# Another order of the steps on all five engines, and PSUM banks that go round the whole program

## The chip, the cores and the metric

The kernel runs on one core of one Trainium2 chip. Five engines work side by side, each through its own list of instructions in order: TensorE (PE in the profile; its weight loads are PEld), VectorE (DVE), ScalarE (ACT), GpSimd (POOL) and SyncE (SP), which here issues every DMA. An instruction starts when the one before it on its engine has gone and the semaphores that it names have reached their values. The metric is the time of one execution in microseconds (us).

## The reference

The input x is 16 batches of 512 tokens by 256 features, float32. For each batch:

```python
xn = layernorm(x)                                   # no gain, no bias
s  = attn(xn)                                       # 16 heads of 16 features
g  = silu(ffn(xn))
x  = x + s * g

# attn, for one batch
v = x @ v_w + v_b
wts = top8_softmax(mean_over_tokens(x) @ gate_w + ...)      # 16 heads x 16 waves
kern = sum(wts * sum(amps * sin(freqs . positions + phases)))
causal_kern = 3.0 * step(kern) * window                     # one row of 512 lags per head
scores = causal_kern[i - j] + qm[i] + km[j] + 0.15 * (qc . kc) / sqrt(8)
ctx = softmax(causal(scores)) @ v
h = layernorm(x + ctx @ out_w + out_b) * g1 + b1
return layernorm(h + gelu(h @ ffn_w1 + b) @ ffn_w2 + b) * g2 + b2

# ffn: three linear layers whose operands are first rounded to FP4 in blocks of 16
h = silu(q(x) @ q(w_gate).T) * (q(x) @ q(w_up).T)           # 704 wide
return q(h) @ q(w_down).T
```

The batches meet nowhere. What they share is prepared once: the statistics and the token means of all 16 batches (all of x has to be read for them), the kernel rows of every head and batch, and the three rounded weights.

## The kernel before

The program has no loop at run time. Python writes every engine's instructions out, from the table ORDER: a list of step names for each engine in three parts. The part `head` opens the program (steps `pre:` once for all, `pro:` for batch 0 ahead of time, `first:` for batch 0), `mid` is written out 14 times for batches 1 to 14, and `end` holds batch 15 (`last:`) and what is left after it (`tail:`). The order of a list is the order on that engine; nothing else schedules.

One batch goes through three stages that overlap with its neighbours. Names in the order lists are those of the code's branches:

- xT, proj, v make the transposed tokens, the split query and key parts and the values of the next batch. SP's `splitio` and `load` send the parts to DRAM and read them back in another layout.
- mx (40 uses of a bank in a batch) finds each row's maximum ahead of time: TensorE at L624, VectorE at L1037. mfin and mT turn the maxima into bias rows.
- sc.p.u is a piece of the scores of head pair p (L654 and L658). ScalarE takes the exponential (L822, L833); VectorE multiplies the near blocks by the kernel row (muld, L1067), GpSimd the far ones (mul, L1176). pv (L674) is the product with the values, ctxe and ctxt normalize it.
- xq, xr, gu, silu, hq, hr, tr, dn are the FP4 network: gu at L701, the rounding on VectorE at L923 to L941 and on GpSimd at L1215 and L1217, tr at L711, dn at L718.
- cT (L725), out (L733), ln1, lnc1, lnb1 (L980), hT (L750), f1 (L760), the Gelu on ScalarE (L913), f2 (L769), ln2 (L958), lnc2, lnb2 and fin end the batch before: they run one batch late.

In the opening, `px.n` loads batch n of x into one of four buffers, `st.n` and `cp.n` take its statistics on VectorE, and `sum` (L1541) adds its token means on TensorE, which frees the buffer for px.n+4. The last sum is L1546. After it comes a chain: pooled, gl, topk, wide, kern (L1585), tanh, soft (L1515 to L1520), the exponential at L1672 and the DMA of the kernel rows. `busy` (L1608) are matmuls of no use that keep TensorE going.

PSUM has eight banks. Scores use 0 and 1. The rest are two rings: 6 and 7 for xT, proj, v, mx and mT (49 uses in a batch), 2 to 5 for all else (56 uses). psum_plan gives each use the next bank of its ring and notes which use had it before; TensorE waits for that one's reader.

Of the kernel before, what the change touches and what calls it, by code (L numbers as in the profile page):

```python
# [56 lines left out]
class Event:  # L57
# [5 lines left out]
    def wait(self, eng, b, k=None):  # L63

        if isinstance(b, int) and b < 0:
# [18 lines left out]
            pro:projm.2 pre:wm.0.0 pre:rs.6 pre:rs.7 pre:rs.8 pre:rs.9 pre:rs.10 pre:wm.0.1 pre:rs.11 pre:rs.12
            pre:wm.1.0 pre:rs.13 pre:rs.14 pre:rs.15 pre:wm.1.1 first:xnb pro:xq pre:wm.2.0 pre:wm.2.1 pro:xr first:xq
            first:projm.0 first:projm.1 first:xr first:projm.2 first:mul.0 first:mul.1 first:hq.0 first:mul.2
            first:hr.0 first:mul.3 first:hq.1 first:mul.4 first:hr.1 first:hq.2 first:mul.5 first:hr.2 first:mul.6
            first:hq.3 first:mul.7 first:hr.3
# [1647 lines left out]
```

How the kernel before makes its waits and increments, by code:

```python
    def wait(self, eng, b, k=None):  # L63
        if isinstance(b, int) and b < 0:
            return
        k = self.per - 1 if k is None else k
        eng.wait_ge(self.sem, b * (self.per * self.by) + (k + 1) * self.by)
# [352 lines left out]
        def inc(ins, name):  # L421
            ins.then_inc(E[name].sem, 1)
# [56 lines left out]
        def sync_steps(sp, part, at_batch):  # L479
# [27 lines left out]
                        cols, r = slice(t * P, (t + 1) * P), 2 * H * t  # L507
                        sp.dma_start(qb_d[:, 3:6, cols], bias_sp[r:r + H]).then_inc(d_split.sem, 16)
                        sp.dma_start(kb_d[:, 0:3, cols], bias_sp[r + H:r + 2 * H]).then_inc(d_split.sem, 16)
                elif k == "load":
                    half = s[1]
                    hb = half_batch(half, b)
                    if which != "pro":
                        E["pe_sc"].wait(sp, hb - 1, 24 * half + 23)
                    if which == "pro":
                        sp.wait_ge(L["filled"], 2)
                        sp.wait_ge(L["ones"], 32)
                    d_split.wait(sp, hb)
                    pairs = slice(HALF * half, HALF * (half + 1))
# [24 lines left out]
                        E["g_mul"].wait(sp, b, p - 2)  # L545
                    else:
                        v_mul[1].wait(sp, b - 1, PAIRS - 2 + p)
                        E["g_mul"].wait(sp, b - 1, PAIRS - 2 + p)
                    if which == "first" and p < 2:
                        sp.wait_ge(L["rows"], 16 * 5)
                    for e in range(2):
                        r = rows_d[b, 2 * p + e, :]
```

## Time and profile before

| | us |
|---|---|
| median of 3 runs | 1924.22 (1918.35 to 1926.29) |
| the profiled execution's own span, first to last instruction | 1916.1 |
| batches 1 to 14, each | 109.82 |

| engine | busy, us | share of the span |
|---|---|---|
| PE | 1822.3 | 95% |
| PEld | 1311.7 | 68% |
| DVE | 1590.4 | 83% |
| POOL | 1095.4 | 57% |
| ACT | 930.2 | 49% |

The 109.82 us of one batch are the distance between two starts of L725, the first matmul of a batch's list. The cT of batch 1 starts 232.45 us into the span and that of batch 15 at 1770.10, so the opening, the 14 middle batches and the end share the span at about 232, 1538 and 146 us. A matmul's row shows its own length and not the pace: the next one starts before it ends. In square brackets at the end of a row is the idle time of the engine before it, and what ended that.

### The profile page before, as it was taken

Reading aid. Unit: us, or ns where it says so; the run is one execution under the profiler, and the core shown is the slowest. Engines: PE = TensorE matmul, PEld = TensorE weight load, DVE = VectorE, ACT = ScalarE, POOL = GpSimd, SP = SyncE. Lnnn points to the kernel's source line nnn. Section 1 sums busy time; section 2 is a strip of 40 time slices with the busy share of each in tenths; the row PEclk is TensorE's granted clock in tenths of the full one; section 3 lists DMA queues with packets and bytes.
Section 4 is the critical chain, followed back from the end, with each engine's and each line's share of the span. In section 5 each row is a group of like instructions: output and inputs, shape, how many; then the busy total and the mean of one; then the engine's idle time right before and its main releaser. Section 6 shows DMA issues by size and latency. Waiting matters only on the chain.

```text
span 1916.1 us, 37547 instructions
## 1 busy us (share of the span) xinstructions
PE 1822.3 (95%) x12803; PEld 1311.7 (68%) x12803; DVE 1590.4 (83%) x5143; ACT 930.2 (49%) x1939; POOL 1095.4 (57%) x797
## 2 busy tenths in 40 slices
...
GB/s 156 165 96 114 64 91 83 75 110 75 99 75 79 76 82 115 75 90 73 91 74 93 93 75 110 64 102 79 83 77 75 110 84 91 75 85 74 61 57 34
DMA packets 138646, 166.69 MB, mean 87 GB/s; under 512 B 19757, under 2 KB 100654, under 8 KB 138452
## 3 DMA queue, kind: packets, MB, share of 16 engines
...
q14 instruction: 84, 0.69, 0.1%
...
## 4 chain that ended last, share of the span: by engine, by line
PE 50%; DVE 26%; issue 12%; POOL 4%; DMA 3%; ACT 3%; SPq 2%; DVEq 0%; POOLq 0%; ACTq 0%
PE ps L760 8%; PE ps L769 7%; PE ps L701 7%; PE ps L718 4%; DVE Pr L1067 3%; PE ps L624 3%; PE ps L597 3%; PE ps L733 3%; PE ps L658 3%; PE ps L674 2%; DVE nmax L1037 2%; POOL slot L1215 2%; PE ps L654 2%; DMA Tz<-kernel_rows 2%; DVE st L958 2%
## 5 line engine op out<-in xcount | busy, mean ns | idle before, releaser
L1176 POOL TENSOR_TENSOR Pr<-Pr,Tz 128x768 f32<-128x768 f32 (+2 forms) x384 | 477.6, 1273 | 233.8 <-ACT Pr L833 230.0
L1037 DVE CUSTOM_DVE_ANT_0 ps<-ps,future 128x512 f32<-128x512 f32 (+3 forms) x1024 | 474.5, 516 | 52.9 <-issue 51.8
L833 ACT ACTIVATE Pr<-ps 128x384 f32<-128x384 f32 x512 | 243.1, 489 | 345.2 <-PE ps L658 343.9
L760 PE MATMUL ps<-catT,w 128*128 128x256 f32 x1024 | 237.8, 380 | 0.7 <-ACT catT L896 0.7
L769 PE MATMUL ps<-w,gT 128*128 128x256 f32 x1024 | 232.9, 381 | 0.9 <-ACT gT L913 0.9
L624 PE MATMUL ps<-KS,QS 108*128 108x512 bf16 (+3 forms) x1024 | 215.0, 300 | 17.9 <-DVE nmax L1037 13.2
L822 ACT ACTIVATE ps<-ps 128x512 f32<-128x512 f32 x256 | 150.5, 588 | 137.7 <-PE ps L654 136.1
L1067 DVE SCALAR_TENSOR_TENSOR Pr<-ps,Tz 128x512 f32<-128x512 f32 x256 | 175.3, 685 | 46.2 <-ACT ps L822 41.0
L769 PEld LDWEIGHTS ps<-w,gT 128*128 128x128 f32 x1024 | 190.8, 190 | 25.7 <-ACT gT L913 1.3
L760 PEld LDWEIGHTS ps<-catT,w 128*128 128x128 f32 x1024 | 189.6, 190 | 26.2 <-ACT catT L896 0.9
L718 PE MATMUL ps<-wdT,hqT 128*128 128x256 f32 x768 | 179.5, 383 | 0.7 <-ACT hqT L872 0.7
L658 PE MATMUL ps<-QS,KS 112*128 112x384 bf16 (+2 forms) x768 | 161.3, 274 | 17.9 <-DVE Pr L1067 12.7
L701 PE MATMUL ps<-wgT,xqT 128*128 128x352 f32 x512 | 175.9, 466 | 0.0
L701 PE MATMUL ps<-wuT,xqT 128*128 128x352 f32 x512 | 172.3, 459 | 0.0
L1215 POOL TENSOR_TENSOR slot<-slot 128x704 f32<-128x704 f32 x64 | 107.7, 1683 | 99.2 <-DVE slot L941 99.2
L1225 POOL TENSOR_TENSOR rstd<-ve,minus_half 128x4 f32<-128x4 f32 (+1 forms) x34 | 33.3, 980 | 222.0 <-DVE ve L966 220.5
L718 PEld LDWEIGHTS ps<-wdT,hqT 128*128 128x128 f32 x768 | 142.9, 191 | 21.2 <-ACT hqT L872 3.5
L674 PE MATMUL ps<-Pr,v_cur 128*17 128x128 f32 (+2 forms) x3584 | 151.0, 319 | 0.0
L624 PEld LDWEIGHTS ps<-KS,QS 108*128 108x128 bf16 x1024 | 87.0, 97 | 91.2 <-DVE nmax L1037 40.8
L1037 DVE DVE_READ_ACCUMULATOR2_ANT nmax<- 128x1 f32 x1024 | 143.2, 140 | 0.0
L701 PEld LDWEIGHTS ps<-wuT,xqT 128*128 128x128 f32 x512 | 97.2, 190 | 54.2
L674 PEld LDWEIGHTS ps<-Pr,v_cur 128*17 128x17 f32 x3584 | 94.5, 97 | 51.4 <-issue 38.7
...
## 6 DMA issues: line engine op xcount, KB each, us to landing
Tz<-kernel_rows SPq DMA_DIRECT2D x256, 256.0 KB, 3.6
...
```

What stands on the lines that cost most here:

```text
L624: ins = mm(o, QS[0:KROWS, 2 * p + e, it * P:(it + 1) * P], KS[0:KROWS, p, 0:n], start=True, stop=True)
L658: ins = mm(dst[:, at:at + PAST[j]], KS[0:SROWS, p, j * P:(j + 1) * P], rhs[:, S - 1:P * (j + 1) - 1:-1], start=True, stop=True)
L674: ins = mm(dst[32 * hh:32 * hh + HD + 1, to:to + n], v_cur[:, j, 4 * g + hh, :], rhs[:, n - 1::-1], start=i == 0, stop=i == len(pieces) - 1)
L701: ins = mm(dst[:, 0:IH], xqT[:, c, t * P:(t + 1) * P], wt[:, c, f * IH:(f + 1) * IH], start=c == 0, stop=c == KD - 1)
L718: ins = mm(dst[:, 0:D], hqT[:, c * P:(c + 1) * P], wdT[:, c, :], start=c == 0, stop=c == KI - 1)
L760: ins = mm(dst[:, i * n:(i + 1) * n], w1[:, c, f * P:(f + 1) * P], catT[:, c, hf * n:(hf + 1) * n], start=c == 0, stop=c == KD - 1)
L769: ins = mm(dst[:, 0:D], gT[:, f, at:at + P], w2[:, f, :], start=f == 0, stop=f == KF - 1)
L822: inc(af(src, src, ACT.Exp), "a_exp")
L833: inc(af(Pr[:, p % 4, e, at:at + wd], src[:, 0:wd], ACT.Exp), "a_exp")
L1037: ins = v.tensor_tensor_reduce(o, o, future[:, S - n:S], -1.0, 3e38, ALU.add, ALU.min, nmax[:, 2 * pl + e, it:it + 1])
L1067: v.scalar_tensor_tensor(blocks(Pr[:, p % 4, e, 0:S]), blocks(ps[:, SC_BANKS[n % len(SC_BANKS)], :]), 3e38, near, ALU.min, ALU.mult).then_ ...
L1176: ins = g.tensor_tensor(a, a, Tz[:, p % 2, :, P * j:P * j + PAST[j]], ALU.mult)
```

## The change

Every list of ORDER gets another order; no step is added or taken out. psum_plan no longer plans the three parts apart and repeats the middle one: it lists the uses of the whole program batch by batch and goes round the ring without a break. With 49 uses and two banks, a batch before began on the bank on which the last one had ended (mT.0, then mx.1.0.0); now they alternate, and every other batch has the two banks swapped. The ring of four is as before in the middle, since 56 is a multiple of 4.

```diff
 ORDER = dict(
     head=dict(
         sync="""
-            pre:px.0 pre:px.1 pre:waves pre:px.2 pro:xload pre:px.3 pre:ld.w_proj pre:ld.w_gate pre:ld.w_v
+            pre:px.2 pre:waves pre:px.0 pre:px.1 pro:xload pre:ld.w_gate pre:ld.w_proj pre:px.3 pre:px.4 pre:ld.c0
...
 PARTS = dict(head=dict(pre=-2, pro=-1, first=0), mid=dict(mid=0), end=dict(last=B - 1, tail=B))
+TURNS = [("head", 0)] + [("mid", b) for b in range(1, B - 1)] + [("end", B - 1)]
...
 def psum_plan(orders, kinds, banks):
...
-    uses = {p: [(w, u) for w, s in orders[p] for u in kinds(s)] for p in PARTS}
-    place, before = {}, {}
-    tail = {p: dict(zip(banks, uses[p][-len(banks):])) for p in PARTS}
-    for b in banks:
-        assert tail["head"].get(b, (0, 0))[1] == tail["mid"][b][1], "banks differ between iterations"
-    for p in PARTS:
-        last = {}
-        if p == "mid":
-            last = {b: (u, -1) for b, (w, u) in tail["mid"].items()}
-        for i, (w, u) in enumerate(uses[p]):
-            bank = banks[(i - len(uses[p])) % len(banks)]
-            place[w, u] = bank
-            at = PARTS[p][w]
-            if p == "end" and bank not in last:
-                before[w, u] = (tail["mid"][bank][1], B - 2 - at)
-            elif bank in last:
-                before[w, u] = (last[bank][0], last[bank][1] - (at if p != "mid" else 0))
-            last[bank] = (u, at)
+    uses = [(at, u) for p, at in TURNS for w, s in orders[p] for u in kinds(s) for at in [at if p == "mid" else PARTS[p][w]]]
+    ahead = sum(len(kinds(s)) for w, s in orders["head"])
+    place, before, last = {}, {}, {}
+    for i, (at, u) in enumerate(uses):
+        bank = banks[(i - ahead) % len(banks)]
+        place[at, u] = bank
+        if bank in last:
+            before[at, u] = last[bank]
+        last[bank] = (u, at)
     return place, before
...
-                earlier, ago = before[which, u]
-                released(eng, earlier, b + ago)
-            return ps[:, place[which, u], :]
+                released(eng, *before[b, u])
+            return ps[:, place[b, u], :]
```

ScalarE in a middle batch, around the second half of the Gelu (gT), before; Pr and ps are exponentials of scores, th a tanh of the FP4 network, and an ACT_TABLE_LOAD brings in the table of the function after it:

```order
L805 ACTIVATE bias_sp<-bias_r 128x128
L872 ACTIVATE hqT<-ps 128x512
L913 ACT_TABLE_LOAD
L913 ACTIVATE gT<-ps,b 128x256 x8
L833 ACT_TABLE_LOAD
L833 ACTIVATE Pr<-ps 128x384
L822 ACTIVATE ps<-ps 128x512
L833 ACTIVATE Pr<-ps 128x384 x2
L862 ACTIVATE th<-ps 128x352
```

and the same place now (lines are 12 lower in the changed file):

```order
L793 ACTIVATE bias_sp<-bias_r 128x128
L901 ACT_TABLE_LOAD
L901 ACTIVATE gT<-ps,b 128x256 x4
L860 ACTIVATE hqT<-ps 128x512
L901 ACTIVATE gT<-ps,b 128x256 x2
L821 ACT_TABLE_LOAD
L821 ACTIVATE Pr<-ps 128x384
L901 ACT_TABLE_LOAD
L901 ACTIVATE gT<-ps,b 128x256 x2
L821 ACT_TABLE_LOAD
L821 ACTIVATE Pr<-ps 128x384
```

The exponential of sc.4.4 now stands between the third and the fourth pair of Gelus, so that four loads stand here instead of two; over the program 94 stand on ScalarE instead of 66, and all 28 more are in the middle batches. The exponentials of sc.4.2 and sc.4.3, which stood behind this block, have moved ahead of it.

TensorE at the start of the program, before; L1554 is `arg`, L1541 `sum`, L587 the transpose of batch 0's tokens, L597 its projections:

```order
L1536 MATMUL ps<-ctxn 16x256
L1554 MATMUL ps<-ctxT,Tz 128x512 x3
L1541 MATMUL ps<-hY,v_cur 16x256 x4
L1554 MATMUL ps<-ctxT,Tz 128x512 x6
L1541 MATMUL ps<-y,v_cur 16x256 x4
L1554 MATMUL ps<-ctxT,Tz 128x512
L587 MATMUL ps<-ident,xn 128x128 x8
L597 MATMUL ps<-xnT,cq 128x512 x2
```

and now:

```order
L1542 MATMUL ps<-ctxT,Tz 128x512 x4
L1524 MATMUL ps<-ctxn 16x256
L1542 MATMUL ps<-ctxT,Tz 128x512 x3
L1529 MATMUL ps<-hY,v_cur 16x256 x4
L1542 MATMUL ps<-ctxT,Tz 128x512 x2
L575 MATMUL ps<-ident,xn 128x128 x8
L1542 MATMUL ps<-ctxT,Tz 128x512
L585 MATMUL ps<-xnT,cq 128x512 x2
```

Seven `arg` now stand ahead of the first sum instead of three, and the transposes of batch 0 ahead of the second sum. On SP, the 16 loads of `basis`, which stood ahead of px.4, now stand behind px.12, and `splitio` ahead of px.8 instead of behind px.9.

TensorE at the end, from the last cT on, before; L711 is tr.3, L718 dn.3, L742 the tail's hT:

```order
L725 MATMUL ps<-ident,ctxn 128x128 x8
L733 MATMUL ps<-ow,catT 128x256 x8
L711 MATMUL ps<-ident,slot 128x128 x6
L718 MATMUL ps<-wdT,hqT 128x256 x6
L742 MATMUL ps<-ident,hY 128x128 x4
```

and now:

```order
L713 MATMUL ps<-ident,ctxn 128x128 x8
L699 MATMUL ps<-ident,slot 128x128 x6
L721 MATMUL ps<-ow,catT 128x256 x4
L706 MATMUL ps<-wdT,hqT 128x256 x6
L721 MATMUL ps<-ow,catT 128x256 x4
L730 MATMUL ps<-ident,hY 128x128 x4
```

tr.3 has moved between the transposes of cT and the product that waits for their copy, and dn.3 between the two halves of that product. On DVE in the same part, ln2 stood ahead of muld.7.0 and hr.3 ahead of muld.7.1; now muld.7.0 and muld.7.1 stand together ahead of both. On GpSimd, hr.3 stands ahead of fin.

## Rows read from the trace of the kernel before

**Rows 1.** The page's first part: busy us, share of the span, instructions.

```profile
PE 1822.3 (95%) x12803; PEld 1311.7 (68%) x12803; DVE 1590.4 (83%) x5143; ACT 930.2 (49%) x1939; POOL 1095.4 (57%) x797
```

**Rows 2.** Timeline of PE in batch 8: start us, us, what, idle before and releaser.

```profile
1001.38 1.04 PE L725 MATMUL ps<-ident,ctxn 128*128 128x128 f32 x8
1003.15 3.72 PE L733 MATMUL ps<-ow,catT 128*128 128x256 f32 x16 [0.74 <-ACT catT L891]
...
1016.65 1.09 PE L750 MATMUL ps<-ident,hY 128*128 128x128 f32 x8 [0.34 <-DVE hY L980]
...
1018.64 0.34 PE L658 MATMUL ps<-QS,KS 112*128 112x256 bf16 x2 [0.51 <-DVE Pr L1067]
...
1020.06 1.89 PE L760 MATMUL ps<-catT,w 128*128 128x256 f32 x8
...
1111.20 1.04 PE L725 MATMUL ps<-ident,ctxn 128*128 128x128 f32 x8
```

**Rows 3.** Windows: busy time of each engine in one batch.

```profile
core 0: us, PE busy (x) PEld busy (x) DVE busy (x) ACT busy (x) POOL busy (x), PEclk, DMA share, GB/s
...
1002.00:1111.60 109.60, 106.87 (x776) 79.14 (x775) 94.18 (x305) 54.05 (x110) 65.42 (x47) 1.00 0.30 86
```

**Rows 4.** Timeline of ACT in batch 8, the second half of the Gelu.

```profile
1053.88 1.28 ACT L913 ACT_TABLE_LOAD   x1
...
1058.45 0.84 ACT L913 ACTIVATE gT<-ps,b 128x256 f32<-128x256 f32 x2 [0.89 <-PE ps L760]
1059.31 1.28 ACT L833 ACT_TABLE_LOAD   x1
1060.60 0.49 ACT L833 ACTIVATE Pr<-ps 128x384 f32<-128x384 f32 x1
```

**Rows 5.** Timeline of DVE in batch 8, its second half.

```profile
1066.07 0.51 DVE L1104 SCALAR_TENSOR_TENSOR slot<-th,ps 128x352 f32<-128x352 f32 x1
...
1067.81 0.69 DVE L1067 SCALAR_TENSOR_TENSOR Pr<-ps,Tz 128x512 f32<-128x512 f32 x1 [0.67 <-DMA Tz<-kernel_rows]
...
1077.71 1.40 DVE L958 BATCH_NORM_STATS2 st<-y 128x6 f32<-128x256 f32 x4
...
1081.61 0.68 DVE L1067 SCALAR_TENSOR_TENSOR Pr<-ps,Tz 128x512 f32<-128x512 f32 x1
```

**Rows 6.** Timeline of PE in the opening.

```profile
14.92 3.59 PE L1541 MATMUL ps<-hY,v_cur 128*16 128x256 f32 x8 [1.72 <-DVE v_cur L1442]
...
30.00 1.09 PE L587 MATMUL ps<-ident,xn 128*128 128x128 f32 x8
...
107.12 1.89 PE L1546 MATMUL ps<-gT 128*16 128x256 f32 x8
```

**Rows 7.** Timeline of SP in the opening (issues of DMAs).

```profile
16.12 5.39 SPq L1340 DMA_DIRECT2D gs<-in_basis_t  x16
21.56 0.40 SPq L1335 DMA_DIRECT2D hY<-in_x  x1
...
88.92 0.37 SPq L1335 DMA_DIRECT2D catT<-in_x  x1
```

**Rows 8.** Timeline of DVE in the opening: the first step of soft.

```profile
143.01 1.73 DVE L1515 TENSOR_SCALAR Tz<-Pr 128x2048 f32<-128x2048 f32 x1
```

**Rows 9.** Timeline of PE in the end: dn.1, sc.7.5, dn.2, the last out, the tail's hT.

```profile
1848.98 2.75 PE L718 MATMUL ps<-wdT,hqT 128*128 128x256 f32 x12
...
1855.07 0.50 PE L658 MATMUL ps<-QS,KS 112*128 112x256 bf16 x2 [1.28 <-DVE Pr L1067]
1855.36 4.19 PE L718 MATMUL ps<-wdT,hqT 128*128 128x256 f32 x12
...
1868.65 1.56 PE L733 MATMUL ps<-ow,catT 128*128 128x256 f32 x6 [0.74 <-ACT catT L891]
...
1876.46 0.60 PE L742 MATMUL ps<-ident,hY 128*128 128x128 f32 x4
```

**Rows 10.** Timeline of DVE in the end: a step of ln2.

```profile
1849.17 1.49 DVE L961 COPY ve<-st 128x4 f32<-128x4 f32 x1
```

More of the change, by code:

```diff
@@ L81 @@
+            pre:px.5 pre:ld.w_v pre:px.6 pre:px.7 pro:splitio pre:px.8 pre:px.9 pre:ld.c1 pre:ones pre:px.10 pro:load.0
+            pre:px.11 pre:px.12 pre:ld.basis pre:px.13 pre:px.14 pre:px.15 pre:ld.c2 pro:load.1 pre:ld.w_rest pro:mio.0
+            first:xload pre:rz pre:rows first:T.0 first:T.1 first:splitio first:T.2 first:T.3 first:mio.1 first:T.4
+            first:load.0 first:T.5 first:T.6 first:T.7 first:mio.0
         """,
         gpsimd="""
-            pre:half pre:rs.0 pre:ones pre:iota pre:rs.1 pre:rs.2 pre:rs.3 pro:projm.0 pre:rs.4 pro:projm.1 pre:rs.5
@@ L84 @@
[L84 to L88, printed above, removed]
+            pre:iota pre:half pre:rs.0 pre:rs.1 pre:ones pre:rs.2 pre:rs.3 pre:rs.4 pro:projm.0 pro:projm.1 pro:projm.2
@@ L113 @@
+            first:mx.0.1.1 first:mx.0.1.2 first:muld.7.0 first:mx.0.1.3 first:mx.0.1.4 first:muld.7.1 first:hq.3
+            first:mx.0.2.0 first:mx.0.2.1 first:mx.0.2.2 first:mx.0.2.3 first:mx.0.2.4 first:dn.1 first:mx.0.3.0
+            first:hr.3 pre:join first:mx.0.3.1 first:mx.0.3.2 first:ctxt.2 first:mx.0.3.3 first:mx.0.3.4 first:dn.2
+            first:mfin.0 first:ctxt.3 first:dn.3
         """,
         tensor="""
-            pre:sum.0 pre:arg.0 pre:arg.1 pre:arg.2 pre:sum.1 pre:arg.3 pre:arg.4 pre:arg.5 pre:arg.6 pre:arg.7
@@ L179 @@
-            mx.0.1.4 hq.3 muld.7.1 mx.0.2.0 mx.0.2.1 mx.0.2.2 mx.0.2.3 mx.0.2.4 dn.1 ctxt.2 hr.3 mx.0.3.0 mx.0.3.1
-            dn.2 mx.0.3.2 mx.0.3.3 mx.0.3.4 mfin.0 ctxt.3 dn.3
+            mx.1.2.2 mx.1.2.3 norm mx.1.2.4 mx.1.3.0 muld.2.1 mx.1.3.1 mx.1.3.2 silu.1.1 mx.1.3.3 mx.1.3.4 muld.3.0
+            mfin.1 hr.0 muld.3.1 f2.0 proj.0 ctxt.0 hq.1 f2.1 proj.1 muld.4.0 proj.2 muld.4.1 xq hr.1 xr v.0 silu.2.0
+            muld.5.0 xr2 silu.2.1 hq.2 f2.2 mx.0.0.0 muld.5.1 hr.2 mx.0.0.1 f2.3 mx.0.0.2 ln2 muld.6.0 mx.0.0.3 lnc2 v.1
```

274 lines of the change are left out of this document (134 added, 140 removed).

## The prediction, made before the changed kernel ran

> **What bounds the kernel now.** I read the page's first part, then the starts of one step batch after batch, then the waits inside one batch, then the two ends. TensorE is busy for 95% of the span and VectorE for 83%; ScalarE and GpSimd are far from full [rows 1]. In a window of 109.60 us, TensorE works 106.87 at a granted clock of 1.00, which is 2.4 GHz, and VectorE 94.18 [rows 3]. From cT to cT a batch takes 1111.20 - 1001.38 = 109.82 us [rows 2], and 14 of them make 1538 of the 1916 us. So TensorE's own work sets the pace there. An order can win only the waits, about 3 us in a batch, while each new wait costs its length 14 times. Opening and end are different: there TensorE waits, or does work of no use, and a chain through SP, VectorE and GpSimd sets the time.
>
> **The banks.** Before, mT.0 and then mx.1.0.0 of the next batch took the same bank. No wait stands there: TensorE sat idle ahead of the product of L733 (for the copy of catT), ahead of L750 (for the layernorm on VectorE) and ahead of a score (for muld) [rows 2]; the rows name no copy of mT's bank. mT.0 is read long before mx.1.0.0, since cT, both out and two gu lie between. The other ring's rotation is the same in the middle. I take 0. Below nothing it can hardly go; above, 0.3 us a batch, about a TensorE wait in these rows, would be 4 us. That the banks alone do nothing is part of my forecast.
>
> **The middle batches, step by step.** I walk through one batch in the new order with the durations of the old trace, 0 being cT's start.
>
> Start: cT, then 0.74 us for the copy, then out. Nothing has moved between them, so this wait stays. The new order puts lnb1 two steps sooner on VectorE, so that hT no longer waits (0.34 us) and sc.1.2, which waited 0.51 for muld.1.0 [rows 2], waits less. Against that, gu.0.1 now stands ahead of sc.0.1 and sc.0.2, and ScalarE has a tanh and both exponentials to do before sc.0.3 and sc.0.4 may write. An exponential takes 0.49 us [rows 4]; I take one and a half of them as new waits, 0.7, and the old waits as the gain, 0.7. The first Gelu matmul, at 1020.06 - 1001.38 = 18.7 us, starts at 18.7 again.
>
> Gelu block: ScalarE gets two more table loads in every batch, since sc.4.4's exponential stands between two pairs of Gelus. One load is 1.28 us, and the next function follows 0.01 us after it [rows 4]. That is 2.6 us more on ScalarE in a batch, whose busy time is 54.05 of 109.60 [rows 3]. What is on the path is what TensorE waits for: sc.5.0 needs sc.4.4's exponential. By the walk that ends at 58.6 us and sc.5.0 comes up at 59.1, because f1.1.2, f1.1.3 and v.0 stand between. The exponential of sc.4.5, behind the fourth load, ends at 62.5; sc.5.1 comes up at 64.0. VectorE's silu.2.0 started at 1066.07, 64.7 us into the batch [rows 5]; its tanh is behind the loads now and ready at 63.4. So the loads hide, by margins of 0.5 and 1.5 us. I take 0. If the cover goes, the bound is 2 x 1.28 = 2.6 us a batch; below nothing they cannot go.
>
> The Trainium skill ("ScalarE: Activation LUTs", What ACT_TABLE_LOAD costs) puts about 1.38 us of drain beside each 1.28 us load. The rows show none: 1059.31 + 1.28 is 1060.59, and the exponential starts at 1060.60 [rows 4]. By that rule both loads ahead of sc.4.4 would make sc.5.0 over 2 us late and the kernel slower; by the row it is on time.
>
> Second half: VectorE's muld.5.0 waited 0.67 us for a kernel row's DMA [rows 5]. projm.1 and projm.2 now stand ahead of hq.1 on GpSimd, so splitio on SP ends sooner, and with it this DMA comes sooner. But ln2 (its first row at 1077.71) still stands ahead of muld.6.0 (1081.61) [rows 5], while sc.6.2, which needs muld.6.0, is now ahead of ctxt.1 and v.1. TensorE comes to it about 1 us before VectorE is through: 0.9 us of new wait. The end of the batch is set as before by VectorE's last mx, mfin.0 and the transposes mT.0: 0.5 us of wait. VectorE has 94.18 us of work in 109.60 [rows 3], almost all of its slack in the first 66 us, so the second half cannot be pulled together much. My walk ends at 109.9 us against 109.82.
>
> Sum of the middle: +0.1 x 14 = +1.4 us, taken as +1. The errors of such a walk are some tenths at each step; I keep -1.2 (all of 0.34, 0.51 and about half of the rest of the waits) to +2.6 (both loads bare) a batch, -17 to +36 us.
>
> **The opening.** Two things move what starts late. On TensorE the first sum waited for VectorE's cp at 14.92, with four `arg` behind it that needed nothing from it; batch 0's transposes came at 30.00, behind the second sum [rows 6]. Now both stand ahead, and cp.0 stands right behind st.0. I expect the transposes at 17 to 20, bounded by the norm, and the projections at about 20, bounded by their weights. On SP px.4 was issued at 21.56, right behind 5.39 us of basis loads [rows 7]; these have gone behind px.12. splitio, 9.6 us of issues, stood ahead of px.10 behind px.8 and px.9; it can now run from about 36 instead of 59, so that px.10 to px.15 come sooner. px.15 was issued at 88.92 [rows 7] and the last sum ran at 107.12 [rows 6], 18 us later. Between that sum and soft at 143.01 [rows 8] VectorE is nearly full with the same steps in both orders, so what the last sum gains passes through, no more. The gain at SP's queue is above 10 us, but px loads, the maxima of batch 0 on VectorE, and the 44 busy matmuls ahead of sum.5 (about 15 us) stand in between. From 0 (all swallowed) to -18 (the whole of px.15's distance); I take -8, near the middle.
>
> **The end.** sc.7.5 waited 1.28 us for muld.7.1 [rows 9], which stood behind ln2 with a step of 1.49 us [rows 10] and hr.3; it goes ahead of both. The twelve matmuls of dn.2 took 4.19 us against 2.75 of dn.1 [rows 9]; with no gap ahead they should run as dn.1 did, 1.4 less. At the last cT, 0.74 us of wait [rows 9] gets tr.3 as filler, 0.65 us of work, and hT.0, at 1876.46 [rows 9], no longer stands behind all of out.1, tr.3 and dn.3 but can start when lnb1.0 is done, some 1.5 us sooner. Sum 1.3 + 1.4 + 1.5 = 4.2; I take -4, from 0 to -6.
>
> **The sum.** 1916.1 - 8 + 1 - 4 = 1905.1 us of span. The median of the runs shown is 1924.2, 8.1 above this span, so 1913.
>
> **The rivals.**
> A: the tables decide. ScalarE's queue from f1.1.0 to silu.2.0 is late, sc.5.0, and through the tanh silu.2.0, muld.5.0 and all that VectorE does to muld.6.0. For it: the margin of 0.5 us, and VectorE is full behind silu.2.0. Against: TensorE has some 3 us of products ahead of sc.5.0. It decides from a lateness of more than 0.5 us. With all 2.6 us bare 1913 + 36 = 1949; with half of it 1931.
> B: the opening gives nothing, as px loads are bound by the DMA engines and VectorE fills the time, and the end gives 2. 1924.2 + 1 - 2 = 1923, no change. For it: SP's queue is not the only thing ahead of the last sum.
> C: my new waits at sc.0.3, sc.6.2 and mT.0 are not there, since VectorE runs ahead after the sooner DMA. Then 1.7 us a batch more is won: 1913 - 24 = 1889. For it: each of them is under 1 us long, less than the walk can be wrong by. Against: VectorE's 94 us.
>
> **How the numbers follow.** Runs of this kernel spread by 0.4%, so about 0.5%, 9.6 us, can be told from no change: below 1914.6 is faster, above 1933.8 slower. Forecast 0.45 (its own range 1903 to 1924; 0.28 of it below 1914.6, 0.17 within), A 0.16 (0.14 slower, 0.02 within), B 0.16 (within), C 0.15 (faster), something else 0.08 (0.03, 0.02, 0.03). Faster 0.46, same 0.37, slower 0.17. C reaches to 1889 and half of A to 1940: 1890 to 1940.
>
> **What would show it.** Batches: L725's starts 109.9 apart; under 108.5 it is C, over 111 it is A. Tables: 94 loads; no row of TensorE waiting for L821's exponential at sc.5.0. New small waits ahead of L646 behind gu.0.1 and behind gu.3.0, none ahead of L738 (hT). Opening: first L575 before 20, px.15 before 80, L1534 near 99, L1503 near 135. End: dn.2 near 2.8 us long. I am wrong if the middle moves by more than 15 us either way or the opening comes later than before.

## The result, and the profile after

The changed kernel takes 2039.34 us (median of 4 runs, 2038.5 to 2041.35), the kernel before 1922.62 us (4 runs on the same chip): a ratio of 1.0609, 95% interval 1.0587 to 1.0632. Forecast were 1913 us, at most 1940. All medians and ratios below leave out two executions, one of e1's ten and one of e7's four, in which TensorE was granted a lower clock from start to end. The loss is in the loop. The mean distance of two cT starts, from batch 1 to batch 15, went from 109.83 to 117.94 us; 14 times 8.11 is 113.5 of the 123.5 us by which the span grew. The rest is opening and end.

The page's first part after, against [rows 1], with the line on the chain that ended last:

```profile
PE 1862.3 (91%) x12797; PEld 1325.3 (65%) x12803; DVE 1665.2 (82%) x5143; ACT 968.9 (48%) x1967; POOL 1138.9 (56%) x797
...
DVE 37%; PE 35%; issue 17%; ACT 8%; DMA 1%; POOL 1%; SPq 0%; DVEq 0%; POOLq 0%; ACTq 0%
```

VectorE executes the same 5143 instructions and is busy for 75 us more. That is the first thing to see: not only waits have grown but the instructions themselves. (In the chain that ended last, before, TensorE had 50% and VectorE 26%.) The groups of the costliest instructions say which, first before and then after (line, shapes, count | busy us, mean ns | idle before):

```profile
L980 DVE SCALAR_TENSOR_TENSOR y<-y,rstd,row_ln_b 128x256 f32<-128x256 f32 x64 | 26.9, 481 | 0.8 <-POOL rstd L1225 0.2
L972 DVE SCALAR_TENSOR_TENSOR y<-y,mv,row_ln_g 128x256 f32<-128x256 f32 x64 | 26.8, 479 | 0.1
```

```profile
L960 DVE SCALAR_TENSOR_TENSOR y<-y,mv,row_ln_g 128x256 f32<-128x256 f32 x64 | 91.1, 1480 | 0.1
...
L968 DVE SCALAR_TENSOR_TENSOR y<-y,rstd,row_ln_b 128x256 f32<-128x256 f32 x64 | 62.4, 1031 | 0.0
```

These are lnc2 and lnb2, the last two steps of the second layernorm: four instructions each in a batch, 99.8 us more in all, 6.2 per batch. Batch 8 shows when (PE's timeline, answering [rows 2], with the three longest waits of its second half):

```profile
1065.62 1.04 PE L713 MATMUL ps<-ident,ctxn 128*128 128x128 f32 x8
...
1080.61 1.04 PE L738 MATMUL ps<-ident,hY 128*128 128x128 f32 x8
...
1082.35 0.34 PE L646 MATMUL ps<-QS,KS 112*128 112x256 bf16 x2
...
1146.23 0.34 PE L646 MATMUL ps<-QS,KS 112*128 112x256 bf16 x2 [0.96 <-DVE Pr L1055]
...
1154.02 0.34 PE L646 MATMUL ps<-QS,KS 112*128 112x256 bf16 x2 [2.47 <-DVE Pr L1055]
...
1161.44 2.36 PE L662 MATMUL ps<-Pr,v_cur 128*17 128x384 f32 x56 [1.87 <-DVE gs L1115]
...
1183.06 1.04 PE L713 MATMUL ps<-ident,ctxn 128*128 128x128 f32 x8
```

The waits at hT and sc.1.2 are gone as forecast, and the first Gelu matmul comes at 18.6 us. The batch is 117.44 us long and loses it behind 80 us: at sc.6.2, at sc.6.5 and at pv.2, each time to VectorE. VectorE at the first of these places, and GpSimd beside it (timelines):

```profile
1146.10 0.56 DVE L1025 CUSTOM_DVE_ANT_0 ps<-ps,future 128x384 f32<-128x384 f32 x1
...
1146.83 5.88 DVE L960 SCALAR_TENSOR_TENSOR y<-y,mv,row_ln_g 128x256 f32<-128x256 f32 x4
...
1155.60 4.12 DVE L968 SCALAR_TENSOR_TENSOR y<-y,rstd,row_ln_b 128x256 f32<-128x256 f32 x4
```

```profile
1146.26 4.08 POOL L1164 TENSOR_TENSOR Pr<-Pr,Tz 128x768 f32<-128x768 f32 x3
1150.31 2.11 POOL L1179 TENSOR_TENSOR catT<-catT,sc_x 128x1024 f32<-128x1024 f32 x1
1154.96 4.08 POOL L1164 TENSOR_TENSOR Pr<-Pr,Tz 128x768 f32<-128x768 f32 x3 [2.54 <-ACT Pr L821]
```

lnc2 lies beside mul.5 and xr, lnb2 beside mul.6. A step between them that reads one operand from PSUM (mx at 1146.10, beside mul.5) keeps its 0.56 us. In the old order VectorE needed 1.67 us for each of the two, and GpSimd was idle then. Windows of one batch before and after, cut at 66 us (columns as in [rows 3]):

```profile
1001.40:1067.40 66.00, 64.04 (x399) 47.30 (x398) 54.12 (x160) 38.73 (x76) 35.17 (x26) 1.00 0.33 97
1067.40:1111.20 43.80, 43.03 (x379) 32.04 (x379) 40.07 (x145) 15.51 (x34) 30.25 (x22) 1.00 0.25 69
```

```profile
1065.40:1131.40 66.00, 64.37 (x399) 47.18 (x398) 51.53 (x162) 40.39 (x77) 34.01 (x25) 1.00 0.40 107
1131.40:1182.80 51.40, 45.13 (x380) 33.06 (x379) 47.50 (x144) 16.52 (x35) 34.33 (x23) 0.97 0.15 45
```

Up to 66 us nothing is lost for TensorE, but VectorE has done 2.6 us less (51.53 against 54.12). In what is left it has 47.50 us instead of 40.07, and the stretch grows from 43.8 to 51.4. TensorE's clock explains little of it. In batch 8 it was granted at 0.50, which is 1.2 GHz, from about 1155.0 to 1158.4, right behind the wait of 2.47 us, and at 2.4 GHz in the rest of the batch. Such a stretch stands in 11 of the 14 batches; these are 118.06 us long on the mean, and the three without one 117.50.

The table loads answer [rows 4] as forecast (ACT's timeline; 94 loads in all):

```profile
1122.60 1.28 ACT L821 ACT_TABLE_LOAD   x1
1123.89 0.49 ACT L821 ACTIVATE Pr<-ps 128x384 f32<-128x384 f32 x1
1124.40 1.28 ACT L901 ACT_TABLE_LOAD   x1
...
1126.55 1.28 ACT L821 ACT_TABLE_LOAD   x1
1127.84 0.49 ACT L821 ACTIVATE Pr<-ps 128x384 f32<-128x384 f32 x1
```

The exponential of sc.4.4 ends 58.8 us into the batch (58.6 forecast), that of sc.4.5 at 62.7 (62.5). No wait of TensorE stands at either.

The opening, answering [rows 6 to 8]: PE and DVE.

```profile
27.02 1.97 PE L575 MATMUL ps<-ident,xn 128*128 128x128 f32 x8
...
102.54 1.67 PE L1534 MATMUL ps<-gT 128*16 128x256 f32 x7
```

```profile
104.81 1.70 DVE L1038 CAST sh_sp<-nmax 128x32 bf16<-128x32 f32 x1
106.55 1.73 DVE L1040 TENSOR_TENSOR sh_sp<-nmax,sh_sp 128x32 bf16<-128x32 f32 x1
108.20 0.18 DVE L1465 COPY pooledT<-ps 128x32 f32<-128x32 f32 x1
...
145.15 1.55 DVE L1503 TENSOR_SCALAR Tz<-Pr 128x2048 f32<-128x2048 f32 x1
```

The transposes come at 27.0 (17 to 20 forecast), the last image of x is issued at 86.66 (before 80), the last sum 4.6 us sooner than before (8 forecast), and soft 2.1 us later (8 sooner forecast). The rows show where much of it went. mfin.0, which now stands ahead of pooledT, took 3.4 us beside GpSimd's products; the same two instructions took 0.39 us before, when GpSimd was idle. TensorE waits 3.23 us for pooledT, and during that wait its clock falls to 0.50, 1.2 GHz, for the stretch in which the small matmuls of the chain come (window, columns as in [rows 3]):

```profile
107.10:120.70 13.60, 10.29 (x29) 3.90 (x31) 10.26 (x50) 6.03 (x10) 6.24 (x3) 0.50 0.01 2
```

The four matmuls behind modT took 1.86 us in it; in the old order they took 1.02, at 2.4 GHz. norm took 3.97 us instead of 1.37, but against that a step of xr, which took 3.18 us beside GpSimd in the old order, took 0.69.

The end, answering [rows 9, 10] (PE):

```profile
1976.10 0.34 PE L646 MATMUL ps<-QS,KS 112*128 112x256 bf16 x2 [1.07 <-ACT hqT L860]
1976.28 2.81 PE L706 MATMUL ps<-wdT,hqT 128*128 128x256 f32 x12
...
1989.32 1.97 PE L713 MATMUL ps<-ident,ctxn 128*128 128x128 f32 x8 [3.10 <-DVE ctxn L1070]
```

dn.2 (1976.28) is 2.8 us long, as forecast, but the last cT waits 3.10 us for VectorE, whose lnc2 and lnb2 of the last batch took 3.13 and 2.46 us beside GpSimd's hr.3. The last step of hr.3, beside mul.7, took 2.53 us instead of 0.89. From batch 15's cT to the last instruction it is 149.3 us, 146.0 before.

### The profile page after: what moved, and what is told of

It is laid out like the page before. It is cut to its first block, busy times and chain, and to the rows that moved or that the text cites. A ratio compares the mean times of both kernels' runs of the same rounds, so it can differ in the third digit from the quotient of the medians.

```text
span 2039.6 us, 37567 instructions
## 1 busy us (share of the span) xinstructions
PE 1862.3 (91%) x12797; PEld 1325.3 (65%) x12803; DVE 1665.2 (82%) x5143; ACT 968.9 (48%) x1967; POOL 1138.9 (56%) x797
## 4 chain that ended last, share of the span: by engine, by line
DVE 37%; PE 35%; issue 17%; ACT 8%; DMA 1%; POOL 1%; SPq 0%; DVEq 0%; POOLq 0%; ACTq 0%
PE ps L748 6%; PE ps L757 5%; DVE Pr L1055 4%; DVE y L960 4%; DVE nmax L1025 3%; DVE ps L1025 3%; DVE y L968 3%; PE ps L585 3%; PE ps L689 3%; PE ps L612 3%; PE ps L721 3%; PE ps L706 2%; PE ps L662 2%; DVE slot L1092 2%; DVE st L946 2%
## 5 line engine op out<-in xcount | busy, mean ns | idle before, releaser
L1164 POOL TENSOR_TENSOR Pr<-Pr,Tz 128x768 f32<-128x768 f32 (+2 forms) x384 | 502.5, 1338 | 216.0 <-ACT Pr L821 215.7
L612 PE MATMUL ps<-KS,QS 108*128 108x512 bf16 (+3 forms) x1024 | 232.1, 304 | 21.0 <-DVE nmax L1025 12.5
L748 PE MATMUL ps<-catT,w 128*128 128x256 f32 x1024 | 242.5, 383 | 0.7 <-ACT catT L884 0.7
L689 PE MATMUL ps<-wgT,xqT 128*128 128x352 f32 x512 | 184.7, 485 | 0.0
L1203 POOL TENSOR_TENSOR slot<-slot 128x704 f32<-128x704 f32 x64 | 121.4, 1897 | 99.6 <-DVE slot L929 99.6
L1197 POOL TENSOR_TENSOR slot<-slot,sc_h 128x704 f32<-128x704 f32 x64 | 88.7, 1386 | 103.5 <-DVE sc_h L918 103.2
```

What stands on the lines that cost most here:

```text
L612: ins = mm(o, QS[0:KROWS, 2 * p + e, it * P:(it + 1) * P], KS[0:KROWS, p, 0:n], start=True, stop=True)
L689: ins = mm(dst[:, 0:IH], xqT[:, c, t * P:(t + 1) * P], wt[:, c, f * IH:(f + 1) * IH], start=c == 0, stop=c == KD - 1)
L748: ins = mm(dst[:, i * n:(i + 1) * n], w1[:, c, f * P:(f + 1) * P], catT[:, c, hf * n:(hf + 1) * n], start=c == 0, stop=c == KD - 1)
L1164: ins = g.tensor_tensor(a, a, Tz[:, p % 2, :, P * j:P * j + PAST[j]], ALU.mult)
```

## The experiments

The first theory was: a VectorE instruction with two inputs in SBUF is held while GpSimd works, that costs 6.6 us a batch, and nothing else does. The first half held in every run; the second did not. "Batch" is the mean distance of two cT starts, batches 1 to 15, of the profiled execution. All ratios are to the kernel before on the same chip.

| | us, median | ratio (interval) | batch, us |
|---|---|---|---|
| before | 1918 to 1926 | 1 | 109.83 |
| after | 2039.3 | 1.0609 (1.0587 to 1.0632) | 117.94 |
| e1 banks | 1918.8 | 0.9994 (0.9977 to 1.001) | 109.82 |
| e2 GpSimd's loop list old | 2066.5 | 1.0759 (1.0729 to 1.0789) | 119.18 |
| e3 GpSimd's loop list new | 2054.7 | 1.0695 (1.0666 to 1.0723) | 119.48 |
| e4 loop old | 1930.5 | 1.0047 (1.0028 to 1.0067) | 109.92 |
| e5 idle products at lnc2 | 1963.6 | 1.0195 (1.0174 to 1.0217) | 112.71 |
| e6 idle products at mx | 1943.2 | 1.0089 (1.0065 to 1.0114) | 111.41 |
| e7 one input | 2028.0 | 1.053 (1.0503 to 1.0558) | |
| e8 apart | 2046.3 | 1.0627 (1.0605 to 1.065) | 118.07 |
| e9 short, new | 2015.7 | 1.0509 (1.0484 to 1.0534) | 116.09 |
| e10 short, old | 1918.5 | 0.9996 (0.9982 to 1.0011) | 109.76 |
| e11 Gelu block | 2054.9 | 1.0708 (1.0673 to 1.0742) | 118.68 |
| e12 apart, second try | 1990.0 | 1.0368 (1.0353 to 1.0384) | 114.06 |
| e13 and xr2 up | 1967.3 | 1.0241 (1.0216 to 1.0266) | 112.80 |
| e14 and v.1 up | 1967.1 | 1.0241 (1.022 to 1.0262) | 112.38 |
| e15 smaller pieces | 2019.2 | 1.0519 (1.0491 to 1.0547) | 116.02 |
| e16 opening mended | 1922.7 | 1.0011 (0.9997 to 1.0024) | 110.16 |
| e17 e14, bank and xr | 1969.3 | 1.0258 (1.0239 to 1.0278) | 112.43 |
| e18 e17, Gelu block | 1985.1 | 1.0347 (1.0325 to 1.0368) | 113.77 |

### Which part of the change costs: e1 to e4

```diff
 e1: psum_plan and bank_for of the changed kernel, ORDER of the old one
 e2: ORDER of the changed kernel, but
-mid gpsimd  ... projm.1 projm.2 hq.1 xq mul.4 hr.1 hq.2 hr.2 ln2 mul.5 xr mul.6 fin ...
+mid gpsimd  ... hq.1 projm.1 hr.1 projm.2 xq xr mul.4 hq.2 mul.5 ln2 hr.2 fin mul.6 ...
 e3: ORDER of the old kernel, but the mid gpsimd list of the changed one
 e4: head and end of the changed kernel, mid of the old one
```

> The old orders of all steps in opening, loop and end, with PSUM banks going round the whole unrolled program. Theory (VectorE is held by GpSimd in the two layernorm steps, 6.6 of the 7.9 us that a batch has grown): banks alone do nothing, batches 109.8 us apart, 1922 us, at most 4 us more. Rival (the banks are what costs): batches 111 to 118 us apart, 1940 us or more.

> The changed kernel, with GpSimd's loop order alone put back to the old one (mul.5 ahead of ln2 and hr.2, xr ahead of mul.4, mul.6 behind fin). Theory (VectorE is held by GpSimd): lnc2 and lnb2 take 1.7 us each again, a batch loses 6.6 of its 117.7 us, about 111 us apart, 1935 to 1965 us in all. Rival (order of TensorE and VectorE, or the two more table loads): lnc2 and lnb2 start as late as now and the time stays above 2025 us.

> All orders old but GpSimd's loop order, which is the new one; banks go round the whole program. Theory (VectorE is held by GpSimd): mul.5 and xr now run when VectorE comes to lnc2 and lnb2, these grow from 3.3 to 6 to 9 us, a batch grows by 3 to 6 us, 1965 to 2010 us. Rival (GpSimd's order costs nothing, it has slack): 1918 to 1930 us.

> New opening and end, old loop on all five engines. Theory: the losses of the three parts add up; batches 109.8 apart, the opening 6.4 us longer and the end 3.6 longer as in the profiled runs, 1932 us. Rival (opening and end gain as I forecast once the loop is not slowed): 1905 to 1915 us.

The banks do nothing (e1). Opening and end cost about 9 us together, and the rest is the loop (e4, as expected). e2's time is the one that its rival named, and e3 cost 45 us more than its range allows. In both the hold is there: e3 has lnc2 at 6.03 us beside xr and mul.6, and in e2 it fell on hr.2 (3.91 us) while lnb2, with GpSimd idle, kept its 1.67. But a list that was not made for the others' lists brings waits of its own, and in both runs TensorE's granted clock is 1.2 GHz for 3.4 or 6.8 us in every one of the 14 batches. The longest wait of e2's VectorE around this place:

```profile
1136.65 0.69 DVE L927 TENSOR_SCALAR hY<-catT 128x1024 uint32<-128x1024 uint32 x1 [5.52 <-POOL catT L1179]
```

To exchange one engine's whole list is therefore no test of the hold. The next runs touch it alone.

### The hold by itself: e5 to e7, e9, e10, e15

```diff
 e5: old orders, in GpSimd's loop ahead of fin (e6: behind hq.0)
+    for i in range(2): g.tensor_tensor(junk[:, 0:3, :], out_b, out_b, mult)
 e7: changed kernel; loop's second layernorm, whose gain and shift are left out
-    scalar_tensor_tensor(y, y, mean, gain, subtract, mult)
+    tensor_scalar(y, y, mean, None, subtract)                # lnb2: times rstd only
 e9: changed kernel (e10: old orders); loop's second layernorm, 248 of 256 columns left out
-    scalar_tensor_tensor(y[:, t, :], y[:, t, :], ...)
+    scalar_tensor_tensor(y[:, t, 0:8], y[:, t, 0:8], ...)
 e15: changed kernel; GpSimd
-    tensor_tensor(a of both heads) x3;      xr: 128x1024 x1
+    tensor_tensor(a of one head) x6;        xr: 128x256 x4
```

> The old orders with two products of 128x768 on GpSimd that nobody reads (inputs a constant row, output a buffer that lies idle), put in front of fin in every batch of the loop, where GpSimd was idle from 83.4 to 86.7 us while VectorE ran lnc2 and lnb2. Theory (a VectorE instruction with two inputs in SBUF is held while GpSimd works): lnc2 and lnb2 together grow from 3.3 to 5 us or more, a batch grows by 1 to 2.5 us, 1936 to 1957 us. Rival (no such hold; what cost was who waits for whom): lnc2 and lnb2 stay at 3.3 us, the time within 5 us of the old one.

> The same two products, put behind hq.0 instead, where GpSimd was idle from 30.4 to 35.8 us and VectorE ran mx steps (one input in PSUM) and norm. Theory: mx steps are not held, norm perhaps; a batch grows by under 0.5 us, 1920 to 1930 us. Rival (more work on GpSimd costs wherever it is): as much as in the other place.

e5's two steps, and GpSimd with the two idle products (DVE, POOL):

```profile
1112.68 4.08 DVE L964 SCALAR_TENSOR_TENSOR y<-y,mv,row_ln_g 128x256 f32<-128x256 f32 x4
...
1116.80 1.67 DVE L972 SCALAR_TENSOR_TENSOR y<-y,rstd,row_ln_b 128x256 f32<-128x256 f32 x4
```

```profile
1112.75 3.33 POOL L1160 TENSOR_TENSOR junk<-row_out_b 128x768 f32<-128x768 f32 x2
1118.55 2.37 POOL L1235 TENSOR_TENSOR y<-y,gs_old 128x1024 f32<-128x1024 f32 x1 [2.46 <-DVE y L972]
```

Work on which nobody waits makes lnc2 2.4 us longer, and a batch 2.9 us longer: the hold is shown, without any other order. Nine of the 14 batches are 112.2 us long, 2.4 more than before, which is just what lnc2 has grown by. The other five are 113.6, and in these TensorE has a stretch of 3.4 us at 1.2 GHz right behind a wait of about 2 us. One batch of each kind (columns as in [rows 3], the seventh figure is the granted clock):

```profile
579.40:691.60 112.20, 107.39 (x778) 79.27 (x777) 96.78 (x305) 54.26 (x110) 68.62 (x49) 1.00 0.31 84
916.10:1029.70 113.60, 108.69 (x778) 79.93 (x777) 96.10 (x305) 54.20 (x110) 68.59 (x49) 0.98 0.30 83
```

Five times 1.3 us is the 6.6 us by which e5 lies above its range. e6 was expected to cost under 0.5 us a batch and cost 1.6, half as much as e5. The mx steps did keep their length, but norm did not (its group in e6; 407 ns before):

```profile
L987 DVE TENSOR_SCALAR xn<-xn,mean_all,rstd_all 128x256 f32<-128x256 f32 x64 | 55.2, 923 | 0.0
```

norm has one input in SBUF and is held all the same. That also answers e7:

> The changed kernel, but lnc2 only subtracts the mean and lnb2 only multiplies by 1/sigma in the loop (gain and shift of the second layernorm are left out): the same waits and the same elements, one input in SBUF instead of two. Theory: both steps are not held any more, 1.7 us each or less in spite of mul.5, xr and mul.6 beside them; batches 110 to 112 us apart, 1930 to 1960 us. Rival (they are slow for another reason, or the wait lies in the orders): batches stay at 117 to 118, 2030 us or more.

e7 won only 11 us. Its form is that of norm, which is held, so it did not take the hold away and tells nothing against it. In its traced execution TensorE's clock was granted at 0.56 throughout, so the length of its batch is not comparable; that VectorE is held can be read there all the same. The step of lnc2, with one input:

```profile
L965 DVE TENSOR_SCALAR y<-y,mv 128x256 f32<-128x256 f32 x56 | 55.8, 1055 | 0.0
```

Beside GpSimd one of these took up to 2.02 us, alone 0.34.

> The changed kernel, with lnc2 and lnb2 of the loop cut to 8 of 256 columns (the rest of the second layernorm is left out): nothing else moves, all waits stay. It takes away their work (3.3 us in the old kernel) and, in the new order, the time for which they are held. Theory (the hold is what the batch has grown by): a batch loses 8 to 9 of its 117.7 us and comes to 108.5 to 110, 1910 to 1935 us in all. Rival (the batch has grown by who waits for whom elsewhere, the long layernorm only fills a wait): it loses 3 us or less, 2000 us or more.

> The same cut in the old orders, to tell what the work of the two steps alone is worth. Both theories: at most 2.6 us a batch, 1885 to 1922 us.

The theory's numbers for e9 failed: a batch lost 1.9 us, not 8 to 9. The rival's numbers came (3 us or less, 2000 us or more), but e9 does not decide for it, since the cut did not take the hold away: lnc2 and lnb2 still took 5.07 and 3.24 us, 1.7 less than the 10.0 of the changed kernel. That run shows best what the hold is. VectorE's four instructions of 8 columns, with the GpSimd instructions beside them (narrow windows of the two timelines, so that a row holds one or two instructions):

```profile
1132.22 1.26 DVE L966 SCALAR_TENSOR_TENSOR y<-y,mv,row_ln_g 128x8 f32<-128x8 f32 x1
...
1132.22 2.49 DVE L966 SCALAR_TENSOR_TENSOR y<-y,mv,row_ln_g 128x8 f32<-128x8 f32 x2
...
1132.22 5.07 DVE L966 SCALAR_TENSOR_TENSOR y<-y,mv,row_ln_g 128x8 f32<-128x8 f32 x4
```

```profile
1131.65 1.81 POOL L1171 TENSOR_TENSOR Pr<-Pr,Tz 128x768 f32<-128x768 f32 x1
...
1131.65 3.03 POOL L1171 TENSOR_TENSOR Pr<-Pr,Tz 128x768 f32<-128x768 f32 x2
...
1135.33 1.93 POOL L1186 TENSOR_TENSOR catT<-catT,sc_x 128x1024 f32<-128x1024 f32 x1
```

GpSimd's first piece ends at 1131.65 + 1.81 = 1133.46, VectorE's first instruction at 1132.22 + 1.26 = 1133.48; the second piece ends at 1134.68 (1131.65 + 3.03), the second instruction at 1134.71 (1132.22 + 2.49); xr ends at 1137.26 (1135.33 + 1.93), the fourth instruction at 1137.29 (1132.22 + 5.07). An instruction of 8 columns that comes up during one of these GpSimd instructions takes as long as what is left of it, and one gets through at each boundary. So the price is set by GpSimd's lengths and by the number of VectorE's instructions, not by VectorE's work; the cut to 8 columns took 1.9 us off a batch instead of 8, and in the old orders, where these two steps are not held, it took nothing (e10). The Trainium skill ("SBUF — State Buffer", Who interferes with whom) has this as a rule: VectorE's second port pair is GpSimd's, whoever comes first keeps it for its whole instruction, and on VectorE it is needed by instructions with two SBUF inputs and by copies, casts and tensor_scalar in the modes that use both ports. By that rule norm and e7 are held too; the traces agree, with 923 ns for norm in e6 against 407 before, and with e7's 1055 ns.

> The changed kernel, all orders as they are, but GpSimd's products in smaller pieces: each product of mul for one head of the pair at a time (6 instructions instead of 3) and xr in four of 256 columns. Theory (a VectorE instruction that comes up during a GpSimd instruction ends when that ends, one gets through at each boundary): the eight instructions of lnc2 and lnb2 take 6.5 to 7.5 us together instead of 10.0, though GpSimd has 0.6 us more to do in each mul; batches 114 to 116 us apart, 1985 to 2015 us. Rival (the two share the port's rate, so pieces change nothing): 10 us or more for the two steps, 2035 us or more.

The same rule, tried from GpSimd's side: in e15 the two steps take 3.59 and 3.62 us, 7.2 together (6.5 to 7.5 expected) against 10.0, though GpSimd's mul is longer. Had the two shared a rate, it would have stayed at 10 us or more (the rival). A batch gets 1.9 us shorter; the total missed its range by 4 us. In 12 of the 14 batches TensorE has a stretch at 1.2 GHz; the two without it are 115.0 us long, 2.5 less than such batches of the changed kernel.

### Keeping the two apart: e8, e12 to e14, e17

```diff
 e8:  mid gpsimd   xq [+xr] mul.4 ... ln2 mul.5 [-xr] [+fin] mul.6 [-fin]
      mid vector   mx.0.0.3 [-lnc2] v.1 muld.6.1 silu.3.0 mx.0.0.4 [+lnc2] lnb2
 e12: as e8, but gpsimd   ln2 mul.5 [+fin] xr mul.6 [-fin]
 e13: e12, and vector     xr [+xr2] v.0 silu.2.0 muld.5.0 [-xr2]
 e14: e13, and tensor     sc.5.1 [+v.1] f2.2;  vector  hq.2 [+v.1] f2.2
 e17: e14, and tensor     mx.0.0.4 [+ctxt.1] dn.0 sc.6.5 [-ctxt.1];  gpsimd  mul.7 [+xr] hr.3
```

> The changed kernel with four moves that keep the two apart: on GpSimd xr behind xq and fin ahead of mul.6, on VectorE lnc2 down to lnb2, both behind mx.0.0.4. Theory: lnc2 and lnb2 run while GpSimd is idle or nearly so, 3.3 to 4.5 us together; batches 110 to 112 us apart, 1930 to 1965 us. Rival (tables or the order on TensorE decide): batches stay above 116 us, 2020 us or more.

> The changed kernel with two moves that keep GpSimd and the two layernorm steps apart and leave xr behind mul.5: fin goes ahead of xr and mul.6 on GpSimd, lnc2 down to lnb2 on VectorE, both behind mx.0.0.4. Theory: 3.3 to 4 us for both steps, batches 110.5 to 113 us apart, 1937 to 1975 us. Rival: above 116 us, 2020 us or more. In e8 the same idea failed, there VectorE waited at hr.2 for GpSimd's hr.1, which stood behind xr; xr stays behind hr.1 here.

e8 failed although lnc2 and lnb2 were back at 1.67 us each. xr, now ahead of mul.4 on GpSimd, waited 7.88 us there for VectorE's xr2; mul.4, hr.1 and hq.2 stand behind it, and VectorE's hr.2 waited for hq.2:

```profile
1141.73 0.53 DVE L927 TENSOR_SCALAR slot<-slot 128x704 uint32<-128x704 uint32 x1 [4.81 <-POOL slot L1202]
```

e12 left xr where it was. Both steps are at 1.67 us (1126.57 and 1128.27 in its trace), and its windows, cut as before, read:

```profile
1040.40:1106.40 66.00, 64.38 (x399) 47.17 (x399) 51.52 (x162) 40.43 (x77) 34.02 (x25) 1.00 0.40 107
1106.40:1154.70 48.30, 43.79 (x381) 32.13 (x380) 42.75 (x144) 16.64 (x35) 33.30 (x23) 1.00 0.16 48
```

VectorE is busy for 94.27 us in the batch, as in the old kernel (94.19), which had some held steps too; a batch is 114.06 us. That is 3.9 us back of 8.1, between the two expectations. No batch of e12, or of e13, e14, e17 and e18, has a stretch at 1.2 GHz; of the 3.9 us about 0.4 are therefore the clock's, an estimate (the changed kernel's mean of 117.94 against its three batches without one, 117.50). The first 66 us still lack VectorE's 2.6 us.

> e12 with one more move: on VectorE xr2 stands right behind xr again, ahead of v.0, silu.2.0 and muld.5.0. In e12 VectorE waited 1.6 us for the tanh at silu.2.0 and then did xr2 beside GpSimd's mul.4, held for 0.9 us. Theory (what is left in e12 is VectorE's lead, given away before 66 us): both come back, a batch loses 1.5 to 2.5 of 114.1 us, 1955 to 1970 us. Rival (what is left sits behind 80 us, at v.1 and pv.2): within 0.5 us of e12 a batch, 1983 us or more.

> e13 with v.1 back behind sc.5.1 on TensorE and behind hq.2 on VectorE. In e12 VectorE had nothing to do for 1.4 us at v.1, whose matmuls stood behind sc.6.2. Theory: another 1 to 1.5 us a batch, 110.5 to 112 us apart, 1935 to 1955 us. Rival: no change against e13.

In the changed kernel and in e12 VectorE waits before silu.2.0 and then does xr2 slowly beside mul.4 (e12's DVE):

```profile
1104.25 0.52 DVE L1097 SCALAR_TENSOR_TENSOR slot<-th,ps 128x352 f32<-128x352 f32 x1 [1.61 <-ACT th L855]
...
1105.85 1.71 DVE L934 TENSOR_TENSOR catT<-catT,hY 128x1024 f32<-128x1024 f32 x1
1107.59 1.63 DVE L937 TENSOR_TENSOR catT<-catT,hY 128x1024 f32<-128x1024 f32 x1
```

With xr2 ahead of that wait the pair takes 1.23 and 1.22 us, a batch 1.3 us less (1.5 to 2.5 expected), and the time is in the expected range (e13). The late v.1 was worth 0.4 us and nothing in the total (e14: the rival).

> e14 with two more moves: on TensorE ctxt.1 ahead of dn.0, so that pv.2 takes the bank that VectorE's ctxt.1 frees and not the one that dn.0 frees, and on GpSimd xr behind mul.7. In e14 pv.2 waited for dn.0 until 89.2 us (ctxt.1 was through at 88.1), and hq.3 was held for a microsecond beside xr and mul.6, with sc.7.5 1.6 us late behind it. Theory (these two waits are the rest): a batch loses 1.8 to 2.4 of its 112.3 us and comes to about 110.2, 1933 to 1943 us. Rival (the rest is spread over the batch): less than 1 us a batch, 1953 us or more.

The wait of pv.2 for dn.0's bank went away, and the batch stayed at 112.43 (the rival again). The hold only moved: xr, behind mul.7, now meets hr.3. DVE in e17:

```profile
1131.13 2.14 DVE L929 TENSOR_SCALAR slot<-slot 128x704 f32<-128x704 f32 x1
```

In e14 it took 0.53 us.

### The table loads: e11, e18

```diff
-mid scalar  f1.1.2 sc.4.4 f1.1.3 sc.4.5     94 loads
+mid scalar  f1.1.2 f1.1.3 sc.4.4 sc.4.5     66 loads
```

> The changed kernel with ScalarE's sc.4.4 put back behind f1.1.3, so that all four Gelus are one block again and 66 table loads are left. Theory: the two loads are hidden, 2030 to 2045 us. Rival A of the forecast (the tables decide): up to 2.6 us a batch less, 2003 us.

> e17 with ScalarE's sc.4.4 back behind f1.1.3 (66 table loads instead of 94). Theory (the two more loads a batch are hidden, sc.5.0 waits for the exponential of sc.4.4 only if that comes behind f1.1.3): slower than e17 by 0.5 to 2 us a batch, since the exponential that sc.5.0 needs comes after the last Gelu at 61.1 us and not at 58.5. Rival A of the forecast: faster by up to 2.6 us a batch.

Rival A of the forecast is out: with 28 loads fewer the kernel is slower, by 0.7 us a batch on the changed kernel and by 1.3 on e17 (the theory for e18). e11 was 10 us above its range, and I did not expect a loss there. In batch 8 of both, TensorE waits 1.01 us at sc.5.0 for the exponential of sc.4.4, which now comes behind the last Gelu; the changed kernel and e17 have no wait there.

### The opening: e16

```diff
 old loop and end; new head, but
-vector  mfin.0 poolT modT ...  kw xr ws.2 norm
+vector  poolT modT mfin.0 ...  kw ws.2 xr norm
-tensor  mx.1.0.4 mT.0 mx.1.1.0 busy.20 arg.15
+tensor  mx.1.0.4 mT.0 arg.15 mx.1.1.0 busy.20
```

> Old loop, old end, and the new opening with three moves put back: on VectorE mfin.0 behind modT and ws.2 ahead of xr, on TensorE arg.15 ahead of mx.1.1.0 and the 16 busy matmuls. Theory (the 4.6 us by which the last sum comes sooner are lost there: mfin.0 held for 3.0 us ahead of pooledT, 1.8 us of wait for arg.15, norm held for 2.6 us): soft starts 7 us sooner than the 145.2 of the changed kernel, near 138, and the time is 1912 to 1925 us. Rival (the new opening is slow elsewhere, in batch 0): soft near 138, but the first cT still at 238 us or later, 1925 us or more.

norm was back at 1.37 us and pooledT came at 106.86, but soft started at 142.74 and not at 138. The matmuls of `wide` stood behind the busy ones as before, and the hold on norm was exchanged for the one on xr: its step took 3.18 us again, as in the old order, where the new one had 0.69. The first cT came at 238.37. The time is that of the old kernel. One execution can't settle the opening: the first cT lay between 232.5 and 240.6 us in six executions with the old opening (mean 236.9) and between 234.5 and 242.5 in twelve with the new (mean 239.5). So the new opening costs about 2.6 us on the mean, not the 6.6 of the first two profiles, and with such a spread even that is uncertain by more than 1 us; what is behind soft was not taken apart.

## Why the prediction was wrong, point by point

**Banks: right.** 0, and e1 says 0.9994.

**The front of the batch: right.** The two waits are gone, 0.39 and 0.37 us of new ones came for the 0.7 forecast, and the first Gelu matmul comes at the forecast time.

**Table loads: right.** 94 loads, both hidden, the two exponentials within 0.2 us of the forecast times, no drain beside a load (1122.60 + 1.28 against 1123.89). What cost there was VectorE's wait for the tanh behind them, 1.6 us, with xr2 put on its wrong side.

**The second half: wrong, and this is the step that failed.** "I walk through one batch in the new order with the durations of the old trace." The durations of lnc2 and lnb2 are those of an idle GpSimd. The walk never put GpSimd's list beside VectorE's, so it gave the two steps 3.3 us where they took 10.0. It forecast 0.9 us of wait at sc.6.2, and behind that only the 0.5 us at mT.0, where 2.47 us came at sc.6.5 and 1.87 at pv.2. That 0.96 us came at sc.6.2 was luck: the forecast put it down to ln2 ahead of muld.6.0, but in e13 these two stand as they did and the wait is gone, so it came from xr2. The bounds were of the walk's errors, "some tenths at each step", -1.2 to +2.6 us a batch; +8.1 lay outside them because a term was missing, not mis-sized. The signs were in the old trace, in rows the prediction used: L961's copy of 1.49 us [rows 10] was read as a step of that length.

**VectorE's slack: seen and not used.** The text said that the second half could not be pulled together since VectorE's slack lay in the first 66 us. In the new order it does 2.6 us less of its work in just these 66 us, and I did not count it; with xr2 and v.1 put back (e14) 1.6 of them return (53.14 us against 51.52).

What the 8.1 us are made of, by the runs: 3.9 the hold at lnc2 and lnb2 with the clock that fell behind it (e12), 1.3 xr2, of whose pair 0.9 were held (e13), 0.4 v.1 (e14). These shares are those of this one sequence of moves. The other 2.5 us are open. In batch 8 of e14 TensorE has two waits that the old order lacks, 1.05 us at pv.2 and 1.24 us at sc.7.5; in e17 they are 0 and 0.69, others have come behind them, and the batch is as long as before.

**Opening: wrong in sign.** The last sum did come sooner, by 4.6 us, but my "passes through" did not hold: mfin.0 was held by GpSimd in the place it had got, TensorE's clock fell to 1.2 GHz in the wait for it, and arg.15 came behind the busy matmuls. norm was held too, but for that xr was not.

**End: wrong in sign.** dn.2 took 2.81 us, as forecast, but not for the reason given, a gap ahead that would go: 1.07 us of gap stand there still. The 4.19 us of [rows 9] belong to that one execution, in which TensorE's clock was at 1.2 GHz from 1854.7 to 1858.2; in the other six executions with the old end dn.2 takes 2.81 us too, so the 1.4 us of the sum were no gain to be had. lnc2 and lnb2 of the last batch moved beside hr.3 and were held, and so was a step of hr.3 beside mul.7. The end takes 149.2 to 151.4 us in twelve executions with the new order and 144.57 in those six, 4.6 to 6.8 less (3.4 in the first two profiles).

**Rivals.** A, B and C were all wrong. The case that came was the 0.08 of "something else", of which 0.03 were for slower, and the range ended 99 us short of it.

None of the 18 kernels of the experiments beats the old one; the old orders with the new bank plan are its equal.
